# Table stage of a graph layer: 64-column score products, 19 row pairs ahead of sort group 1, and a new split of the row scaling between GpSimd and ScalarE

## The chip, the cores and the metric

One Trainium2 chip, one core of it. The metric is the device time of one execution in microseconds (us), taken as the median of several runs.

## What is computed

The reference is a graph layer followed by a feed-forward (slice attention) layer. There are 6250 nodes with 256 features and 106250 weighted edges, sorted by destination in the input arrays. What the change touches is the first half of the graph layer:

```python
support = layernorm(x) @ W
r_D = sigmoid(support @ a2)
gated = r_D * support
out = segment_sum(gated[col] * edge_values[:, None], row, num_segments=n)
sumnorm = segment_sum(edge_values * r_D[col, 0], row, num_segments=n)
```

All that follows (the division, the gating with softplus, the feed-forward layer) is untouched. Because the product with W is linear, the kernel leaves it to the end of the sum. It first builds a **table** with one row of 257 numbers for each node: the normalized features times the gate `r_D`, and the gate itself. It then gathers rows of that table for the edges and adds them up by destination.

## The kernel before

The 6250 rows are kept in on-chip memory as 49 blocks of 128 rows (`NB = 49`), and 25 pairs of blocks (`NPAIR`). Two things are made before the gathering can start, and they run interleaved on all engines.

**The table stage.** For each pair `p`:
- TensorE transposes the two blocks (`cross1`, L1823, four transposes that the profile puts under L1831), ScalarE copies them out of PSUM (`crossed1`, L1558, copy at L1563), and TensorE multiplies them with one column of weights (`support`, L1835), which gives one score for each row. These score products have one moving column; the profile puts them under the helper's line, L1766, as `bank<-S 128x1`. A pair has eight such records, as each float product is two.
- The pairs form four **chunks** (`CUTS`, L70): pairs 0 to 6, 7 to 12, 13 to 18 and 19 to 24, that is 14, 12, 12 and 11 blocks. For a chunk, VectorE scales the scores (`opened`, L1024, its product at L1027), ScalarE takes an exponential (`weight`, L1565, L1568), and VectorE turns them into gates, gains and shifts (`closed`, L1029, L1032 to L1035).
- Each block is then scaled by its gains into a ring of 18 row buffers, `Gt` (`GB = 18`, L67): even blocks by ScalarE (`scaled`, L1570, L1577 and L1578), odd ones by GpSimd (`scaled`, L781, L791 and L792). SyncE stores the blocks in their order, 0 to 48, to the table in DRAM (L641), and waits for each block's scaler. A block 18 or more reuses the buffer of the block 18 before it, so its scaler first waits until the **whole chunk** of that block is stored (`stored`, L568).

**The sort stage** sorts the edges into lists by destination block, in 26 groups of 32 columns. A group `g` goes through VectorE (`lookup` L992, `flag` L958, `place` L1012, `values` L974, `quad` L998, `later` L984, `hot` L1005, `mark` L969, in that order), TensorE (`quads` L1782, `total` L1808, `above` L1769, `other` L1778, and the two halves of `put`, L1793) and ScalarE (`runs_out` L1545 at L1550, `front` L1528 at L1533, `weigh` L1535 at L1542). GpSimd sends the result to DRAM by an indirect DMA (`send`, L756, L765). `other(g + 1)` on TensorE needs `front(g + 1)`, stands ahead of both halves of `put(g)`, and `lookup(g + 1)` on VectorE needs it too. `quads(g)` and `send(g - 1)` need `runs_out(g - 1)`.

**The order by hand.** The first 13 pairs (`FIRST`, L66) go through TensorE ahead of group 1 (L1897), the other twelve are spread over groups 1 and 2, six to a group, at six slots `pair(g, 0)` to `pair(g, 5)`. On VectorE, `pair` (L1037) opens chunk `g` at `(g, 0)` and closes it at `(g, 2)`, for g = 1, 2, 3; chunk 0 is opened and closed ahead of group 1, between the row statistics (L1098) and the second part of the reciprocal roots (`scales(1)`, L1111), which waits for ScalarE's `guess1(1)` (L1552). On ScalarE, after the first pairs, come `weight(0)` and `guess1(1)`, and then for each group:

```python
                pair(g, 0)
                if g > 1:
                    runs_out(g - 1)
                pair(g, 1)
                front(g + 1)
                for i in range(2, PER):
                    if i == 3:
                        weigh(g, 1)
                    pair(g, i)
```

Its `pair` (L1581) scales its half of chunk `g - 1` in the slots from `(g, 2)` on, and chunk 3 at `(3, 5)`. GpSimd's program is `send(0)`, chunks 0 and 1, `send(1)`, chunk 2, `send(2)`, chunk 3, `send(3)`.

**The end of the stage.** When `send(0)` to `send(3)` have landed, and behind the 49 stores in its queue, SyncE loads the first lists (`heads`, L644, L649). VectorE decodes them at the start of group 5 (`decode1`, L1148, L1143), and GpSimd begins to fetch table rows with them (`fetch1`, L769, L777). From there sorting of the later groups and a first pass of gathering and adding run together to about 550 us, and the rest of the gathering and the feed-forward layer follow.

Of the kernel before, what the change touches and what calls it, by code (L numbers as in the profile page):

```python
# [31 lines left out]
P = 128  # L32
N = 6250
F = 256
# [28 lines left out]
GS = (4, 10)  # L63
G1 = GS[0]
PER = 6
FIRST = 13  # L66
GB = 18  # L67
STARTS = (G1 + 1, 12)
NPAIR = -(-NB // 2)
CUTS = (0, 7, FIRST, FIRST + PER, NPAIR)  # L70
NCH = len(CUTS) - 1
assert FIRST + 2 * PER >= NPAIR
WG = 3
H = 8
G = 64
# [3 lines left out]
GW = F + 1  # L79
# [30 lines left out]
def build(nc, x, src, dst, ew, W, a1, a2, W_fx, b_fx, W_x, b_x, W_slice, b_slice, W_q, W_k, W_v,  # L110
          W_out, b_out, temp, out, gtab, srt, ovs):
    with ExitStack() as ctx:
# [305 lines left out]
        s_gt = [sem(f"s_gt{k}") for k in range(2)]  # L418
# [140 lines left out]
        def chunk(j):  # L559
            return 2 * CUTS[j], min(NB, 2 * CUTS[j + 1])  # L560

        def chunk_of(b):
            return sum(b // 2 >= c for c in CUTS) - 1

        def score_bank(j):
            return bank[7 - 4 * (j % 2)]

# [53 lines left out]
        def _(sp):  # L621
# [15 lines left out]


            for b in range(NB):
                sp.wait_ge(s_gt[b % 2], b // 2 + 1)  # L640
                sp.dma_start(gtab[b * P:(b + 1) * P, :], Gt[:, b % GB, :]).then_inc(s_gd[chunk_of(b)], 16)  # L641


# [99 lines left out]
        def _(pool):  # L743
# [12 lines left out]
            def send(g):  # L756
                k = g % 2
                if g == 0:
                    pool.wait_ge(s_zdma, 32)
                else:  # L760
                    pool.wait_ge(s_run, g * 16)
                pool.wait_ge(s_idx0, g + 1)
                pool.wait_ge(s_out, g + 1)
                pool.sem_inc(s_tick, 1)
                pool.indirect_dma_start(  # L765
                    srt[:, :], bass.IndirectOffsetOnAxis(ap=idx[:, k:k + 1], axis=0),
                    runs[k], None).then_inc(s_run, 16)
# [13 lines left out]
            def scaled(j):  # L781
                lo, hi = chunk(j)
                pool.wait_ge(s_gr, j + 1)
                pool.sem_inc(s_tick, 1)
                for b in range(lo, hi):
                    if b % 2 == 0:
                        continue
                    if b >= GB:
                        pool.wait_ge(*stored(chunk_of(b - GB)))
                        pool.sem_inc(s_tick, 1)  # L790
                    pool.tensor_copy(Gt[:, b % GB, F:GW], gate[:, b:b + 1])  # L791
                    pool.tensor_scalar(Gt[:, b % GB, 0:F], res[:, b, :], mean[:, b:b + 1], gain[:, b:b + 1],  # L792
                                       ALU.subtract, ALU.mult).then_inc(s_gt[1], 1)

            send(0)
            scaled(0)
            scaled(1)
            send(1)
            scaled(2)
            send(2)  # L800
            scaled(3)
            send(3)


# [95 lines left out]
        def _(dve):  # L900
# [123 lines left out]
            def opened(j):  # L1024
                lo, hi = chunk(j)
                dve.wait_ge(s_gm, CUTS[j + 1])
                v.tensor_tensor(score[:, lo:hi], score_bank(j)[:, lo:hi], nrs[:, lo:hi], ALU.mult).then_inc(s_g1, 1)  # L1027
# [7 lines left out]
                v.scalar_tensor_tensor(shift_[:, lo:hi], mean[:, lo:hi], -1.0, gain[:, lo:hi], ALU.mult, ALU.mult).then_inc(s_gr, 1)  # L1035

            def pair(g, i):  # L1037
                if g < NCH:
                    if i == 0:
                        opened(g)  # L1040
                    if i == 2:
                        closed(g)

            def dots():
                dve.wait_ge(s_w, 16 * len(wloads))
# [471 lines left out]
        def _(act):  # L1517
# [52 lines left out]
            def scaled(j, lo, hi):  # L1570
                act.wait_ge(s_gr, j + 1)
                for b in range(lo, hi):
                    if b % 2 == 1:
                        continue
                    if b >= GB:
                        act.wait_ge(*stored(chunk_of(b - GB)))
                    a.copy(Gt[:, b % GB, F:GW], gate[:, b:b + 1])  # L1577
                    a.activation(Gt[:, b % GB, 0:F], res[:, b, :], ACT.Identity,  # L1578
                                 bias=shift_[:, b:b + 1], scale=gain[:, b:b + 1]).then_inc(s_gt[0], 1)

            def pair(g, i):  # L1581
                if g < NCH and i == 1:
                    weight(g)
                if turn_of(g, i) < NPAIR:
                    crossed1(turn_of(g, i))
                if g < NCH:
                    lo, hi = chunk(g - 1)
                    if i >= 2:
                        scaled(g - 1, lo + (hi - lo) * (i - 2) // 4, lo + (hi - lo) * (i - 1) // 4)
                if g == NCH - 1 and i == PER - 1:  # L1590
                    scaled(g, *chunk(g))

            def evac(ns):
                for n in ns:
# [29 lines left out]
            for n in range(FIRST):  # L1624
# [2 lines left out]
                    runs_out(0)  # L1627
                if n == 4:
                    guess1(0)
            weight(0)  # L1630
            guess1(1)
            for g in range(1, G1 + 1):
                pair(g, 0)
                if g > 1:
# [129 lines left out]
        def _(pe):  # L1764
# [70 lines left out]
            def support(p):  # L1835
                j = chunk_of(2 * p)
                pe.wait_ge(s_pc, p + 1)
                if j >= 2:
                    pe.wait_ge(s_g1, j - 1)
                for k, b in enumerate(blocks(p)):  # L1840
                    o = score_bank(j)[:, b:b + 1]
                    mm(o, xT1[:, p % 2, k * F:k * F + P], Wg[:, 0, F:GW], True, False)
                    m = mm(o, xT1[:, p % 2, k * F + P:(k + 1) * F], Wg[:, 1, F:GW], False, True)
                m.then_inc(s_gm, 1)

            def step1(n):
# [353 lines left out]
```

## Time and profile before

| | us |
|---|---|
| median of 3 runs | 1389.09 |
| lowest and highest | 1387.78, 1393.01 |
| the profiled execution's own time | 1378.09 |
| its span, first to last instruction | 1376.3 |
| TensorE, VectorE, GpSimd, ScalarE busy | 1191.1, 1027.6, 881.7, 564.2 |

The rows further down are from the profiled execution. Times are us from the start of its span. An engine's row gives start, duration, engine, line, operation, the tiles written and read, their shapes and how many instructions were merged; in brackets stands how long the engine was idle before, and what ended the wait. The "granted clock" of TensorE is a share of its full speed of 2.4 GHz: 1.00 is 2.4 GHz and 0.50 is 1.2 GHz. Busy TensorE time includes time at either clock.

### The profile page before, as it was taken

How to read it: one execution, taken by the hardware profiler on the slowest of the kernel's cores; microseconds unless marked ns; L12 is line 12 of the kernel's file. 1: busy time of each engine (PE TensorE's matmuls, PEld its weight loads, DVE VectorE, ACT ScalarE, POOL GpSimd, SP SyncE). 2: the span in 40 equal slices, each digit the busy share in tenths (PEclk: the TensorE clock that was granted, in tenths of full speed). 3: DMA queues.
4: the chain of work that ended last, by engine and by line, in shares of the span. 5: the costliest groups of instructions: out<-in, count | busy, mean ns of one | idle time of the engine just before them, and what ended most of it. 6: DMA issues, size and time to landing. Idle time of an engine off the chain costs nothing.

```text
span 1376.3 us, 22834 instructions
## 1 busy us (share of the span) xinstructions
PE 1191.1 (87%) x6533; PEld 950.6 (69%) x6533; DVE 1027.6 (75%) x2618; ACT 564.2 (41%) x2046; POOL 881.7 (64%) x894
## 2 busy tenths in 40 slices
PE   3977688888888989789999998989898999988998
PEld 2976577787777888466766666656565666656887
DVE  8777899999898997717787776777777777775222
ACT  3254355555554445003444444443443434443232
POOL 0068777777777777767777777777777777760000
PEclk9677799999999999769999999999999999999999
DMA  8023455665555555736544446544444444441122
GB/s 268 19 70 100 68 150 150 145 165 138 146 147 144 154 135 142 141 93 124 132 129 121 128 130 119 135 120 127 122 128 124 125 126 119 128 112 36 39 76 72
DMA packets 163712, 166.74 MB, mean 121 GB/s; under 512 B 84709, under 2 KB 136185, under 8 KB 163596
## 3 DMA queue, kind: packets, MB, share of 16 engines
q0 software_dynamic: 39712, 108.02, 30.2%
q1 hardware_dynamic: 102716, 37.97, 11.8%
q10 hardware_dynamic: 21168, 19.35, 4.6%
q8 instruction: 54, 0.88, 0.3%
q14 instruction: 62, 0.51, 0.1%
HBM read 137.12 MB, written 28.14 MB: 120 GB/s over the span
## 4 chain that ended last, share of the span: by engine, by line
PE 47%; POOL 12%; issue 11%; DMA 10%; DVE 10%; ACT 8%; POOLq 1%; SPq 0%; ACTq 0%; DVEq 0%
PE bank L1766 45%; POOL rows L874 10%; DMA rows<-gated_rows_dram,ring_i 7%; ACT big L1542 5%; DMA overflow_sums_dram<-ovr 1%; POOL rows L792 1%; ACT big L1708 1%; DVE S L1330 1%; POOLq L866 1%; PE bank L2011 1%; PE bank L1831 1%; DVE lg L1359 1%; DVE big L963 1%; DVE hm L1354 1%; DVE neg L1371 1%
## 5 line engine op out<-in xcount | busy, mean ns | idle before, releaser
L1766 PE MATMUL bank<-rows,S 128*128 128x257 f32 (+1 forms) x2254 | 584.6, 392 | 58.2 <-DMA rows<-gated_rows_dram,ring_i 40.3
L874 POOL DMA_INDIRECT rows<-gated_rows_dram,ring_i x516 | 504.4, 977 | 165.6 <-issue 141.4
L1766 PEld LDWEIGHTS bank<-rows,S 128*128 128x128 f32 x2254 | 409.2, 193 | 183.9 <-DMA rows<-gated_rows_dram,ring_i 79.1
L777 POOL DMA_INDIRECT rows<-gated_rows_dram,lg x294 | 288.7, 982 | 99.8 <-issue 73.4
L1766 PE MATMUL bank<-big 128*104 128x128 f32 (+3 forms) x1824 | 227.1, 288 | 69.6 <-ACT big L1542 50.0
L1766 PEld LDWEIGHTS bank<-big 128*104 128x104 f32 (+2 forms) x1824 | 221.6, 193 | 79.8 <-issue 78.1
L1542 ACT ACTIVATE big<-big 128x52 f32<-128x52 bf16 x768 | 180.0, 324 | 13.6 <-ACT ovr L1601 13.6
L1330 DVE TENSOR_SCALAR S<-iota,lof,srec 128x128 f32<-128x128 f32 x588 | 163.3, 359 | 1.8
L1766 PE MATMUL bank<-xn,lg 128*128 128x256 f32 x392 | 100.1, 379 | 0.0
L1766 PE MATMUL bank<-Wxs,xT 128*128 128x512 f32 x196 | 97.2, 618 | 0.3 <-ACT xT L1695 0.3
L1601 ACT COPY ovr<-bank 128x257 f32<-128x257 f32 x98 | 36.1, 369 | 149.3 <-PE bank L1766 132.8
L1157 DVE TENSOR_SCALAR S<-iota,lg,srec 128x128 f32<-128x128 f32 x294 | 84.0, 360 | 4.5 <-PE bank L1766 3.0
L1766 PE MATMUL bank<-big,lg 128*128 128x128 bf16 (+3 forms) x623 | 60.6, 247 | 28.6 <-DVE big L966 13.3
L1766 PEld LDWEIGHTS bank<-xn,lg 128*128 128x128 f32 x392 | 74.1, 190 | 10.7 <-issue 0.5
L1009 DVE TENSOR_TENSOR big<-bank,lg 128x2048 f32<-128x2048 f32 (+1 forms) x40 | 75.4, 1884 | 0.0
L1371 DVE SCALAR_TENSOR_TENSOR neg<-ag,bc,a1b 128x256 f32<-128x256 f32 x49 | 23.8, 486 | 67.6 <-ACT ag L1660 67.6
L1766 PEld LDWEIGHTS bank<-big,lg 128*128 128x128 bf16 x623 | 47.9, 103 | 37.9 <-DVE big L963 12.9
L1341 DVE TENSOR_TENSOR ag<-bank,ovr 128x257 f32<-128x257 f32 x49 | 20.9, 426 | 67.7 <-PE bank L1766 42.5
L1507 DVE TENSOR_TENSOR S<-bank,res 128x256 f32<-128x256 f32 x49 | 20.8, 425 | 64.6 <-PE bank L1766 64.6
L1708 ACT ACTIVATE big<-bank,zcol 128x128 f32<-128x128 f32 (+1 forms) x196 | 68.2, 356 | 0.0
L1682 ACT ACTIVATE xn<-res,bc 128x256 f32<-128x256 f32 x49 | 29.4, 600 | 88.3 <-DVE bc L1397 88.3
L765 POOL DMA_INDIRECT sorted_edges_dram<-big,idx x26 | 30.7, 1182 | 53.5 <-issue 51.9
(271 smaller groups left out, 1547.0 us busy)
## 6 DMA issues: line engine op xcount, KB each, us to landing
overflow_sums_dram<-ovr ACTq DMA_DIRECT2D x98, 128.5 KB
rows<-gated_rows_dram,ring_i POOLq DMA_INDIRECT x516, 3.2
gated_rows_dram<-rows SPq DMA_DIRECT2D x49, 128.5 KB, 3.1
ovr<-overflow_sums_dram SPq DMA_DIRECT2D x49, 128.5 KB, 2.9
rows<-gated_rows_dram SPq DMA_DIRECT2D x49, 128.5 KB
out_dram<-S SPq DMA_DIRECT2D x48, 128.0 KB, 1.7
rows<-gated_rows_dram,lg POOLq DMA_INDIRECT x294, 3.1
res<-in_x_dram SPq DMA_DIRECT2D x1, 4352.0 KB
```

The lines of the kernel that those rows point to most:

```text
L765: pool.indirect_dma_start(srt[:, :], bass.IndirectOffsetOnAxis(ap=idx[:, k:k + 1], axis=0), runs[k], None).then_inc(s_run, 16)
L777: pool.indirect_dma_start(rows[:, turn(n), :], None, gtab[:, :], bass.IndirectOffsetOnAxis(ap=ring1[:, n:n + 1], axis=0)).then_inc(s_row[t ...
L874: pool.indirect_dma_start(rows[:, slot(b, u), :], None, gtab[:, :], bass.IndirectOffsetOnAxis(ap=ring_i[:, b // CH % 2, n:n + 1], axis=0)) ...
L1009: v.tensor_tensor(hot_s[h], r.unsqueeze(2).broadcast_to([P, HC, RUN[h]]), iota1[:, 0:RUN[h]].unsqueeze(1).broadcast_to([P, HC, RUN[h]]), A ...
L1157: v.tensor_scalar(S[:, turn(n), :], iota[:, :], lof1[:, n:n + 1], srec[:, 1, n:n + 1], ALU.is_equal, ALU.mult).then_inc(s_S, 1)
L1330: v.tensor_scalar(S[:, S_slot(b, u), :], iota[:, :], lof[:, b // CH % 2, n:n + 1], srec[:, 1, NT1 + b * TQ + u:NT1 + b * TQ + u + 1], ALU. ...
L1371: step(v.scalar_tensor_tensor(neg[:, :], ag[:, 0:F], col(RI), a1b[:, :], ALU.mult, ALU.mult, accum_out=col(ZD)))
L1542: m = a.activation(hot_v[h][:, j, 1, :], flagsj[g % 2][:, h, j, :], ACT.Copy, scale=ewf[:, n:n + 1])
L1601: a.copy(ovr[:, k, :], bank[6 + k][:, 0:GW]).then_inc(s_evac, 1)
L1682: a.activation(xn[:, b % 3, :], res[:, b, :], ACT.Identity, bias=col(NM), scale=col(RS)).then_inc(s_xn, 1)
L1708: m = a.activation(swt[:, c, b * P:b * P + n], turn_bank(b)[:, c * P:c * P + n], ACT.Identity, bias=zcol[:, 0:1], accum_out=nacc[:, c, b:b ...
L1766: return nc.tensor.matmul(o, l, r, start=start, stop=stop, skip_group_check=True)
```

## The change

- Score products have 64 moving columns (`WIDE`) in place of one: the same column of weights, read 64 times. The 63 further columns are overwritten by later blocks or not read.
- 19 pairs go through TensorE ahead of sort group 1, and the last six in group 1. The chunks stay as they are.
- VectorE opens chunks 1, 2 and 3 at `(1, 0)`, `(1, 3)` and `(2, 3)` and closes each two slots later; ScalarE's exponentials stand one slot after each opening. `weight(0)` and `guess1(1)` move up among the first pairs, behind pairs 12 and 16.
- GpSimd scales blocks 0 to 25 (chunks 0 and 1), ScalarE blocks 26 to 48 (chunks 2 and 3): chunk 2 in halves at `(2, 0)` and `(2, 1)`, chunk 3 in thirds at `(3, 0)`, `(3, 1)` and `(3, 2)`.
- GpSimd's program is now `send(0)`, chunk 0, `send(1)`, chunk 1, `send(2)`, `send(3)`.

```diff
@@ -63,13 +63,17 @@
 GS = (4, 10)
 G1 = GS[0]
 PER = 6
-FIRST = 13
+FIRST = 19
 GB = 18
+WIDE = 64
 STARTS = (G1 + 1, 12)
 NPAIR = -(-NB // 2)
-CUTS = (0, 7, FIRST, FIRST + PER, NPAIR)
+CUTS = (0, 7, 13, 19, NPAIR)
 NCH = len(CUTS) - 1
-assert FIRST + 2 * PER >= NPAIR
+SCALED = {(2, 0): (2, 0, 2), (2, 1): (2, 1, 2),
+          (3, 0): (3, 0, 3), (3, 1): (3, 1, 3), (3, 2): (3, 2, 3)}
+OPENED = ((1, 0), (1, 3), (2, 3))
+assert FIRST + PER >= NPAIR
 WG = 3
 H = 8
 G = 64
@@ -562,6 +566,13 @@
         def chunk_of(b):
             return sum(b // 2 >= c for c in CUTS) - 1
 
+        def lent_pool(b):
+            return b < 2 * CUTS[2]
+
+        def scaler(b):
+            k = int(lent_pool(b))
+            return s_gt[k], sum(int(lent_pool(c)) == k for c in range(b + 1))
+
         def score_bank(j):
             return bank[7 - 4 * (j % 2)]
 
@@ -637,7 +648,7 @@
 
 
             for b in range(NB):
-                sp.wait_ge(s_gt[b % 2], b // 2 + 1)
+                sp.wait_ge(*scaler(b))
                 sp.dma_start(gtab[b * P:(b + 1) * P, :], Gt[:, b % GB, :]).then_inc(s_gd[chunk_of(b)], 16)
 
 
@@ -783,7 +794,7 @@
                 pool.wait_ge(s_gr, j + 1)
                 pool.sem_inc(s_tick, 1)
                 for b in range(lo, hi):
-                    if b % 2 == 0:
+                    if not lent_pool(b):
                         continue
                     if b >= GB:
                         pool.wait_ge(*stored(chunk_of(b - GB)))
@@ -794,11 +805,9 @@
 
             send(0)
             scaled(0)
+            send(1)
             scaled(1)
-            send(1)
-            scaled(2)
             send(2)
-            scaled(3)
             send(3)
 
 
@@ -1035,11 +1044,10 @@
                 v.scalar_tensor_tensor(shift_[:, lo:hi], mean[:, lo:hi], -1.0, gain[:, lo:hi], ALU.mult, ALU.mult).then_inc(s_gr, 1)
 
             def pair(g, i):
-                if g < NCH:
-                    if i == 0:
-                        opened(g)
-                    if i == 2:
-                        closed(g)
+                if (g, i) in OPENED:
+                    opened(1 + OPENED.index((g, i)))
+                if (g, i - 2) in OPENED:
+                    closed(1 + OPENED.index((g, i - 2)))
 
             def dots():
                 dve.wait_ge(s_w, 16 * len(wloads))
@@ -1570,7 +1578,7 @@
             def scaled(j, lo, hi):
                 act.wait_ge(s_gr, j + 1)
                 for b in range(lo, hi):
-                    if b % 2 == 1:
+                    if lent_pool(b):
                         continue
                     if b >= GB:
                         act.wait_ge(*stored(chunk_of(b - GB)))
@@ -1579,16 +1587,14 @@
                                  bias=shift_[:, b:b + 1], scale=gain[:, b:b + 1]).then_inc(s_gt[0], 1)
 
             def pair(g, i):
-                if g < NCH and i == 1:
-                    weight(g)
+                if (g, i - 1) in OPENED:
+                    weight(1 + OPENED.index((g, i - 1)))
                 if turn_of(g, i) < NPAIR:
                     crossed1(turn_of(g, i))
-                if g < NCH:
-                    lo, hi = chunk(g - 1)
-                    if i >= 2:
-                        scaled(g - 1, lo + (hi - lo) * (i - 2) // 4, lo + (hi - lo) * (i - 1) // 4)
-                if g == NCH - 1 and i == PER - 1:
-                    scaled(g, *chunk(g))
+                j = SCALED.get((g, i))
+                if j is not None:
+                    lo, hi = chunk(j[0])
+                    scaled(j[0], lo + (hi - lo) * j[1] // j[2], lo + (hi - lo) * (j[1] + 1) // j[2])
 
             def evac(ns):
                 for n in ns:
@@ -1627,8 +1633,10 @@
                     runs_out(0)
                 if n == 4:
                     guess1(0)
-            weight(0)
-            guess1(1)
+                if n == 12:
+                    weight(0)
+                if n == 16:
+                    guess1(1)
             for g in range(1, G1 + 1):
                 pair(g, 0)
                 if g > 1:
@@ -1838,9 +1846,9 @@
                 if j >= 2:
                     pe.wait_ge(s_g1, j - 1)
                 for k, b in enumerate(blocks(p)):
-                    o = score_bank(j)[:, b:b + 1]
-                    mm(o, xT1[:, p % 2, k * F:k * F + P], Wg[:, 0, F:GW], True, False)
-                    m = mm(o, xT1[:, p % 2, k * F + P:(k + 1) * F], Wg[:, 1, F:GW], False, True)
+                    o = score_bank(j)[:, b:b + WIDE]
+                    mm(o, xT1[:, p % 2, k * F:k * F + P], Wg[:, 0, F:GW].broadcast_to([P, WIDE]), True, False)
+                    m = mm(o, xT1[:, p % 2, k * F + P:(k + 1) * F], Wg[:, 1, F:GW].broadcast_to([P, WIDE]), False, True)
                 m.then_inc(s_gm, 1)
 
             def step1(n):
```

## Rows read from the trace of the kernel before

**Rows 1.** Chain that ended last, 60 to 165 us: start, us, what
```profile
103.94 6.39 PE bank L1766 x32
...
123.88 4.82 POOL rows L792
...
143.81 3.35 DMA sorted_edges_dram<-big,idx
...
147.60 2.05 DMA srec<-sorted_edges_dram
```

**Rows 2.** Timeline of TensorE, 46 to 92 us: transposes, and a half of put
```profile
46.17 0.60 PE L1831 MATMUL bank<-ident,res 128*128 128x128 f32 x4
...
48.71 0.64 PE L1831 MATMUL bank<-ident,res 128*128 128x128 f32 x4
...
58.91 1.09 PE L1831 MATMUL bank<-ident,res 128*128 128x128 f32 x4
...
61.37 1.09 PE L1831 MATMUL bank<-ident,res 128*128 128x128 f32 x4
...
88.12 3.14 PE L1766 MATMUL bank<-big 128*104 128x80 f32 x32
```

**Rows 3.** Stretches: us; PE, PEld, DVE, ACT, POOL busy; granted clock; DMA; GB/s
```profile
50.00:51.00 1.00, 1.00 (x12) 1.00 (x11) 0.91 (x5) 0.34 (x1) 0.00 (x0) 1.00 0.00 0
...
52.00:53.00 1.00, 1.00 (x7) 1.00 (x6) 0.00 (x0) 0.00 (x0) 0.00 (x0) 0.50 0.00 0
```

**Rows 4.** Timeline of VectorE, 53 to 150 us
```profile
53.20 0.17 DVE L1027 TENSOR_TENSOR big<-bank,big 128x14 f32<-128x14 f32 x1 [1.81 <-PE bank L1766]
...
65.68 0.17 DVE L1032 TENSOR_SCALAR big<-big 128x14 f32<-128x14 f32 x1 [3.78 <-ACT big L1568]
...
69.03 1.89 DVE L994 TENSOR_TENSOR big<-big,bank 128x1664 bf16<-128x1664 bf16 x1
...
93.46 0.17 DVE L1027 TENSOR_TENSOR big<-bank,big 128x12 f32<-128x12 f32 x1 [7.06 <-PE bank L1766]
...
101.51 3.69 DVE L1009 TENSOR_TENSOR big<-big,lg 128x2048 f32<-128x2048 f32 x2
...
107.23 1.89 DVE L994 TENSOR_TENSOR big<-big,bank 128x1664 bf16<-128x1664 bf16 x1
116.04 0.17 DVE L1027 TENSOR_TENSOR big<-bank,big 128x11 f32<-128x11 f32 x1 [6.92 <-PE bank L1766]
...
149.77 0.17 DVE L1143 CAST big<-srec 128x8 int32<-128x8 f32 x1 [3.70 <-DMA srec<-sorted_edges_dram]
```

**Rows 5.** Timeline of GpSimd, 97 to 112 us
```profile
97.89 0.36 POOL L791 COPY rows<-big 128x1 f32<-128x1 f32 x1 [10.84 <-DMA gated_rows_dram<-rows]
...
101.28 4.84 POOL L792 TENSOR_SCALAR rows<-res,big 128x256 f32<-128x256 f32 x1
...
108.64 1.09 POOL L765 DMA_INDIRECT sorted_edges_dram<-big,idx  x1 [0.20 <-issue]
109.75 0.19 POOL L791 COPY rows<-big 128x1 f32<-128x1 f32 x1
...
111.10 0.17 POOL L791 COPY rows<-big 128x1 f32<-128x1 f32 x1
```

**Rows 6.** The stores of the table (writers of its tensor), 60 to 150 us
```profile
DMA to landing us min/median/max: 2.1/3.1/4.7
```

**Rows 7.** Timeline of ScalarE in group 2, 94 to 105 us
```profile
94.44 0.27 ACT L1550 COPY big<-bank 104x128 f32<-104x128 f32 x1
...
98.35 0.34 ACT L1533 CAST big<-bank 128x208 bf16<-128x208 f32 x1
...
99.64 0.19 ACT L1577 COPY rows<-big 128x1 f32<-128x1 f32 x1
...
100.23 0.17 ACT L1577 COPY rows<-big 128x1 f32<-128x1 f32 x1
...
100.82 3.74 ACT L1542 ACTIVATE big<-big 128x52 f32<-128x52 bf16 x16
```

## The prediction

> **What bounds the kernel now.** I read the chain of waits first, for the stretch that the change touches, and then one engine's timeline at a time. In the chain [rows 1] the sort's products on TensorE (32 records, 6.39 us) carry it through group 2. From 116 us on GpSimd's scaling carries it, one block of it 4.82 us long. Then comes send(3), 3.35 us from issue to landing at 147.2, and the load of the first lists. VectorE's timeline [rows 4] shows what that means: it waits 7.06 us for TensorE before it opens chunk 2, 6.92 us before it opens chunk 3, 3.78 us for the exponential of chunk 0, and at 149.77 us it decodes the first lists, 3.70 us late. All that comes after (the later sort groups, the gathering) starts from that decode and has no tie to anything earlier, so I take the time of the decode as the measure: each us it moves is a us of the whole. The reader is to see two things more. Pairs of blocks go through TensorE at two speeds [rows 2]: two pairs in 2.54 us at 46 us, 1.27 each, and one in 2.46 us at 59 us. In both the engine is busy without a gap, and what differs is the granted clock, 1.00 and then 0.50 [rows 3], 2.4 and 1.2 GHz. And GpSimd needs 1.35 us for a block when undisturbed (109.75 to 111.10), but 4.84 us for the one that overlaps VectorE's 3.69 us of `hot` [rows 4, 5].
>
> **Wide products and the first 19 pairs.** The one-column products of a pair go at the pace of their weight loads; a half of put with 80 columns and weights of 104 takes 3.14/32 = 0.098 us a record [rows 2], so 64 columns should fit under the load of 128 weights, and I cost them at 0. If that cover were missing, each of a pair's eight records would add its own excess over that load; no row shows one, and nothing speaks for a gain. Whether they hold the clock no row shows. The bounds are the put's case, full clock at 88 us, and the one-column case, half clock from 52 us. I take full clock, as 64 columns are nearer to 80 than to one. Then pairs 3 to 18 start at 46.17 and take 16 x 1.27 = 20.3 us, plus a last product, to about 67.5.
>
> - Chunk 0 is opened when pair 6 is through, at 52.3 in place of 53.2. The statistics behind it take 61.90 - 53.20 = 8.7 us [rows 4] (61.90 is 65.68 less its wait), to 61.0. The exponential stands behind pair 12 on ScalarE, at 46.17 + 9 x 1.27 + 1.2 (transposes, copy) = 58.8, so the 3.78 us wait is gone. Chunk 0 is closed by 61.8 (0.8 us, as before).
> - What is late next is `guess1(1)`, behind pair 16: 46.17 + 13 x 1.27 + 0.6 (transposes) + 1.1 (copy and two logarithm steps) = 64.5. From there to the end of lookup(1) VectorE needs what it needs now, 70.92 - 65.68 - 0.8 = 4.4 us: 69.0 in place of 70.9. **Gain 1.9 us.**
>
> **Group 1.** VectorE does a group in 15.7 us without its wait (93.46 to 109.12) [rows 4], here 0.8 more for a second closing, and it no longer waits 7.06 us for a chunk at the group's start: lookup(2) ends at 69.0 + 15.7 + 0.8 = 85.5. TensorE's pairs 19 to 24 end by about 92.
>
> **The scaling of chunk 0.** All 14 blocks are now GpSimd's, from 62.0. Undisturbed they need 14 x 1.35 = 18.9 us. Nine blocks took it from 66.7 (the closing of chunk 0) to 87.05 (97.89 less 10.84) [rows 5], 20.3 us with all of VectorE's group 1 beside them, so group 1 blocks GpSimd for 20.3 - 12.2 = 8.1 us. Group 2's flag and values now fall in the same stretch; I estimate 4.7 us from their share. The bounds are no blocking at all and twice the second share. I take 62.0 + 18.9 + 12.8 = 93.7, and 3.1 us and a little for the last store [rows 6]: chunk 0 is stored at 97.2.
>
> **ScalarE's first wait.** At `(2, 0)` it scales blocks 26 to 31, into buffers of chunk 0, so it waits until 97.2. Six blocks at 0.59 (99.64 to 100.23) [rows 7] are 3.5 us. Behind them stands `runs_out(1)`, 0.27 us, now done at 94.71 and then at 101.0: **6.3 us later**. For it wait quads(2) on TensorE and send(1) on GpSimd.
>
> **ScalarE's second wait, the core of my forecast.** At `(2, 1)` it scales blocks 32 to 37, into the buffers of blocks 14 to 19, and so waits for all of chunk 1 to be stored. But chunk 1 is GpSimd's, stands in its queue behind send(1), and send(1) waits for `runs_out(1)`, which ScalarE has just done. So from 101.0: send(1) 1.1 to 1.4 us (108.64 to 109.75) [rows 5], twelve blocks 16.2 us, 3.7 us in which `hot(2)` blocks GpSimd [rows 4], the last store 3.1 us [rows 6]: 125.4. The six blocks add 3.5 us, and only then comes `front(3)`, 0.34 us, done at 129.3. Now it is done at 98.69, 4 us after `runs_out(1)`; then it is 28 us after it. Behind it stand on ScalarE `weigh(2, 1)`, 3.74 us [rows 7], and the exponential of chunk 3 (0.2 us); on TensorE other(3) and both halves of put(2); on VectorE the closing of chunk 3 and lookup(3). VectorE's chain is 129.3 + 3.7 + 0.2 + 0.8 (closing) + 2.0 + 1.9 (mark and lookup) = 137.9. Now lookup(3) ends at 109.12 [rows 4]. **Loss so far 28.8 us.**
>
> **What comes back.** Group 3 has no 6.92 us wait and no closing: 15.7 - 0.8 = 14.9, to 152.8, against 116.04 + 15.66 = 131.7 now (the same group's length). Loss 21.1. TensorE's put(2), 6.4 + 3.1 from 129.4, and put(3) end ahead of what VectorE asks of them, so their clock costs nothing here. Group 4 now takes from 131.7 to 146.07 (149.77 less the wait of 3.70), 14.4 us, with 0.9 of waiting for send(2), which then lands early: 13.5, to 166.3. The lists are then there: put(3) ends about 157, send(3) follows at once as nothing stands ahead of it in GpSimd's queue, and 3.35 us and 2.4 us more (143.81 to 149.65) [rows 1] make 163. So the decode starts at 166.3 against 149.77. **Sum: 16.5 us slower**, of which 1.9 + 7.1 + 6.9 + 0.9 + 3.7 = 20.5 were gained and 37 lost in two waits. The profiled execution would take 1378.09 + 16.5 = 1394.6. The median is 11.0 us (0.8%) above it, and the forecast for the median is 1389.09 + 16.5 = 1405.6.
>
> **Rules weighed.** GpSimd's 4.84 us block began 0.23 us before `hot` at 101.51 [rows 4, 5] and was held up all the same. The Trainium skill (SBUF — State Buffer, Who interferes with whom) says that GpSimd and a VectorE instruction with two inputs in SBUF share a read port, that the one that starts first holds it to its end, and that ScalarE waits for nobody. That speaks against this change, which moves blocks from ScalarE to GpSimd; the trace agrees that GpSimd is the one to suffer, but not that the first to start is safe. By the rule the caught block would lose nothing, and the sum would be 0.4 us shorter. TensorE is busy 1.00 in both stretches of [rows 3], with the clock at 1.00 and at 0.50. The skill (TensorE: Matmul & The Clock Gate, Why this matters for your kernels) says that an engine kept continuously busy gets its full clock; the trace disagrees. By that rule alone, the wide columns would change nothing.
>
> **The rivals.**
> - *The clock falls all the same.* The pairs then take 2.46 us from 52 us on. For it speaks that half of a pair's work is still the same transposes. Against it, the put's case. Pair 16 comes 11 us later, lookup(1) ends at 84, group 1's put and the pairs behind it at 102, and `runs_out(1)` at 105.8 rather than 101.0; the rest follows: 4.8 us more, 1410.4.
> - *Faster: the second wait finds its chunk stored.* If the twelve blocks of chunk 1 were stored when ScalarE comes to `(2, 1)`, which decides at 101 us, nothing would hold front(3). VectorE would run groups 2 and 3 back to back and the lists would set the end; the gains, less the late `runs_out(1)`, are some 14 us: 1375. Against it stands the order of GpSimd's queue: chunk 1 can't start before send(1).
> - *No difference: the loss is made up.* VectorE and GpSimd might meet less than I took. With no blocking at all in chunk 0, TensorE's pairs (92) and ScalarE's six blocks set `runs_out(1)` to 95.5, 5.5 us earlier, and `hot(2)` gives 3.7 back: 7.3 us slower are left, 1396.4. Only with some slack after 150 us as well would it be a draw, about 1392. The chain [rows 1] shows no such slack, with VectorE, lists and GpSimd in line.
> - *Worse.* If GpSimd's blocks of chunk 1 took half as long again as undisturbed, 8 us more: 1414.
>
> **How the numbers follow.** I give the forecast 0.70, the fallen clock 0.12, worse 0.06, no difference 0.08 and faster 0.04. A measurement of this kernel tells about 0.5% (6.9 us) from no change. The range goes from the unblocked case to the worst one, 1396 to 1414, and leaves out the two cases that aren't slower and some of the edges. Faster by over 0.5% 0.04, within it 0.09, slower 0.87.
>
> **What would show it.** In the profile after: a granted clock of 1.00 from 50 to 68 us and 1.27 us a pair; no waits of VectorE of 7 us for its opening products (L1027's line of before) in groups 2 and 3; ScalarE's longest wait, 24 us, on a store of the table ahead of the second half of chunk 2, with TensorE and VectorE idle from about 108 to 129 us; GpSimd's twelve blocks in that stretch at 1.35 us each; the first lists decoded at 166 us without a wait for their DMA, and every later stage late by the same amount. It would be wrong if front(3) came within 10 us of `runs_out(1)`, if lookup(3) ended before 125 us, or if the delay at the decode were gone by the end of the first pass at 550 us.

## The result, and the profile after

| | before | changed |
|---|---|---|
| median of 20 runs, us | 1386.71 | 1391.45 |
| lowest and highest | 1378.9, 1393.01 | 1387.8, 1398.21 |
| the profiled execution's own time | 1378.09 | 1392.19 |
| its span | 1376.3 | 1390.4 |

The ratio is 1.0041, with a 95% interval of 1.0025 to 1.0057: about 5 us slower, within the 0.5% that I had called no change, and below the 1396 at which my range began. I had forecast 16.5 us slower. Yet between the two profiled executions the difference is 14.1 us, near the forecast. So there are two questions: whether the 14 us arise as I said, and why only 5 of them are left between the medians.

The pages give the granted clock in 40 slices of 35 us, first for the kernel before, then for the changed one:

```profile
PEclk9677799999999999769999999999999999999999
```

```profile
PEclk9985889999999999868999999999999999999999
```

The second and third slices (35 to 104 us), most of the table stage, now have 9 and 8 where they had 6 and 7; the 5 behind them is the long wait that follows below. The timeline of TensorE in the first 19 pairs:

```profile
48.72 0.61 PE L1839 MATMUL bank<-ident,res 128*128 128x128 f32 x4
49.16 1.00 PE L1774 MATMUL bank<-S 128*128 128x64 f32 x8
...
64.03 0.61 PE L1839 MATMUL bank<-ident,res 128*128 128x128 f32 x4
...
65.31 0.61 PE L1839 MATMUL bank<-ident,res 128*128 128x128 f32 x4
```

A pair takes 1.28 us at 64 us as at 48, where [rows 2] have 2.46 us at 59. The 64-column products cost nothing that counts: eight of them are busy 1.00 us, eight of one column 0.95 us, and at full clock a pair takes 1.28 us with either.

Then ScalarE, which answers to [rows 7] (start, duration, engine, line and tiles as ahead of the prediction):

```profile
96.56 0.19 ACT L1585 COPY rows<-big 128x1 f32<-128x1 f32 x1 [4.33 <-DMA gated_rows_dram<-rows]
...
100.08 0.24 ACT L1558 COPY big<-bank 104x128 f32<-104x128 f32 x1
124.08 0.19 ACT L1585 COPY rows<-big 128x1 f32<-128x1 f32 x1 [23.76 <-DMA gated_rows_dram<-rows]
...
127.60 0.31 ACT L1541 CAST big<-bank 128x208 bf16<-128x208 f32 x1
```

Both waits that I forecast are there: 4.33 us for the stores of chunk 0, then `runs_out(1)` (L1558) at 100.1, then 23.76 us for the stores of chunk 1, and `front(3)` (L1541) ends at 127.9. GpSimd, to [rows 5]:

```profile
101.33 1.09 POOL L776 DMA_INDIRECT sorted_edges_dram<-big,idx  x1 [6.92 <-ACT big L1558]
102.44 0.19 POOL L802 COPY rows<-big 128x1 f32<-128x1 f32 x1
...
120.55 1.21 POOL L803 TENSOR_SCALAR rows<-res,big 128x256 f32<-128x256 f32 x1
```

Send(1) goes out when `runs_out(1)` is done, and the twelve blocks follow it, to 121.8. VectorE, to [rows 4]:

```profile
66.97 0.20 DVE L1123 TENSOR_TENSOR big<-big 128x35 f32<-128x35 f32 x1 [3.72 <-ACT big L1564]
...
69.71 1.89 DVE L1003 TENSOR_TENSOR big<-big,bank 128x1664 bf16<-128x1664 bf16 x1
...
102.47 0.56 DVE L1010 TENSOR_REDUCE big<-bank 128x32 f32<-128x384 f32 x1 [8.91 <-PE bank L1774]
...
131.70 0.17 DVE L1041 TENSOR_SCALAR big<-big 128x11 f32<-128x11 f32 x1 [22.93 <-ACT big L1576]
...
134.38 1.89 DVE L1003 TENSOR_TENSOR big<-big,bank 128x1664 bf16<-128x1664 bf16 x1
...
163.65 0.17 DVE L1151 CAST big<-srec 128x8 int32<-128x8 f32 x1
```

Its two waits of 7 us are gone. Two of 8.9 us (for `quads(2)`, behind `runs_out(1)`) and 22.9 us (for the exponential of chunk 3, behind `front(3)`) have come, and the first lists are decoded at 163.7 without waiting for them. From there to the end of the program both profiled executions need the same: the own times less the decode are 1228.3 us before and 1228.5 after.

### The profile page after: what moved, and what is told of

Same layout as the page of the kernel before. It is cut to its first block, busy times and chain, and to the rows that moved or that the text cites. A ratio compares the mean times of both kernels' runs of the same rounds, so it can differ in the third digit from the quotient of the medians.

```text
span 1390.4 us, 22822 instructions
## 1 busy us (share of the span) xinstructions
PE 1186.4 (85%) x6533; PEld 948.3 (68%) x6533; DVE 1029.6 (74%) x2618; ACT 563.5 (41%) x2042; POOL 874.0 (63%) x898
## 4 chain that ended last, share of the span: by engine, by line
PE 42%; POOL 14%; DVE 11%; issue 11%; DMA 11%; ACT 8%; POOLq 1%; SPq 0%; ACTq 0%; DVEq 0%
PE bank L1774 40%; POOL rows L883 10%; DMA rows<-gated_rows_dram,ring_i 7%; ACT big L1550 5%; POOL rows L803 3%; DMA overflow_sums_dram<-ovr 2%; ACT big L1716 1%; DVE S L1338 1%; PE bank L2019 1%; POOLq L875 1%; DVE big L1018 1%; DVE big L988 1%; DVE big L972 1%; DVE big L979 1%; DVE lg L1367 1%
## 5 line engine op out<-in xcount | busy, mean ns | idle before, releaser
L1774 PE MATMUL bank<-big 128*104 128x128 f32 (+3 forms) x1824 | 230.7, 291 | 65.9 <-ACT big L1550 51.2
L1774 PEld LDWEIGHTS bank<-big 128*104 128x104 f32 (+2 forms) x1824 | 225.4, 196 | 75.0 <-issue 73.4
L1774 PE MATMUL bank<-big,lg 128*128 128x128 bf16 (+3 forms) x623 | 57.6, 240 | 57.0 <-ACT big L1541 25.3
L1774 PE MATMUL bank<-xn,lg 128*128 128x256 f32 x392 | 101.0, 382 | 0.0
L776 POOL DMA_INDIRECT sorted_edges_dram<-big,idx x26 | 32.8, 1262 | 91.4 <-issue 52.9
```

Of the source, the lines that this page charges most:

```text
L776: pool.indirect_dma_start(srt[:, :], bass.IndirectOffsetOnAxis(ap=idx[:, k:k + 1], axis=0), runs[k], None).then_inc(s_run, 16)
L1774: return nc.tensor.matmul(o, l, r, start=start, stop=stop, skip_group_check=True)
```

## The experiments

**Both kernels again.** The first question was what an ordinary execution of either kernel looks like.

> The kernel before, unchanged, profiled a second time. The first profile had the first lists decoded at 149.8 us and a time of 1378.1, while 20 runs spread from 1378.9 to 1393.0 around 1386.7. Theory A (the spread is made in the first 150 us, where six pairs of blocks and the sort products ran at half clock for a time that varies, and they set the pace there): another profile has the decode anywhere from 149 to 164 us and its own time moves with it, so that time minus decode stays within 2 us of 1228.3. Rival B (the spread is made later, in the gathering): the decode stays at 149.8 within 1 us and the time moves without it.

> The changed kernel, unchanged, profiled a second time. Its first profile had the decode at 163.7 us; its 20 runs spread less (1387.8 to 1398.2). Theory A (its first 150 us hang on GpSimd's and ScalarE's chain, not on TensorE's clock): decode at 163.7 within 1.5 us, time 1388 to 1394. Rival B: the decode stays too, and the time can be anywhere in the spread.

> The kernel before, unchanged, a third profile. The first two had the decode at 149.8 and 156.7 us, own times of 1378.1 and 1385.2, and a clock that rose again from 0.50 at 75 and at 90 us. Theory A (TensorE's clock in the first 100 us decides): the decode lies between 149 and 160 us, later the longer the clock stays at 0.50 between 33 and 100 us, and time minus decode is 1227 to 1232. Its usual value must be near 156, so that the median of some 1388 comes out. Rival B: a decode near 150 with a time above 1384.

> As before_3: a fourth profile of the kernel before, with the same expectations of both theories.

> The changed kernel, unchanged, a third profile. The first two had the decode at 163.7 and 164.7 us. Theory A (its first 150 us don't hang on the clock): 163 to 166 us again. Rival: a spread as wide as that of the kernel before, 7 us.

| kernel, profile | opening of chunk 2 | first decode | own time | own time less decode |
|---|---|---|---|---|
| before, first | 93.5 | 149.8 | 1378.1 | 1228.3 |
| before_2 | 97.4 | 156.7 | 1385.2 | 1228.5 |
| before_3 | 98.1 | 156.4 | 1395.8 | 1239.5 |
| before_4 | 97.2 | 157.1 | 1392.6 | 1235.5 |
| changed, first | | 163.7 | 1392.2 | 1228.5 |
| after_2 | | 164.7 | 1396.8 | 1232.1 |
| after_3 | | 164.0 | 1394.7 | 1230.7 |

The first profile of before, on which my prediction rests, differs from the other three, which have the decode 6.6 to 7.3 us later. How common each kind is, four profiles don't tell: of the 20 timed runs of before, six took 1378.9 to 1380.5 us and nine less than 1385, so executions as quick as that profile are not rare. The changed kernel's three profiles lie within 1.1 us at the decode. What differs shows in the table stage. The stretch from 33 to 100 us, in the first profile of before:

```profile
33.00:100.00 67.00, 61.03 (x430) 57.33 (x431) 50.84 (x118) 22.83 (x65) 23.59 (x23) 0.74 0.14 45
```

in before_2:

```profile
33.00:100.00 67.00, 63.59 (x394) 60.04 (x391) 46.89 (x107) 21.18 (x60) 21.47 (x19) 0.65 0.13 44
```

and in the changed kernel's first:

```profile
33.00:100.00 67.00, 53.84 (x450) 51.92 (x450) 51.16 (x118) 22.87 (x62) 32.14 (x29) 0.89 0.14 46
```

The column before the last two is the granted clock: 0.74, 0.65, 0.89. TensorE's timeline in before_2 tells where:

```profile
77.41 1.06 PE L1831 MATMUL bank<-ident,res 128*128 128x128 f32 x4
...
79.83 1.09 PE L1831 MATMUL bank<-ident,res 128*128 128x128 f32 x4
...
84.76 6.19 PE L1766 MATMUL bank<-big 128*104 128x128 f32 x32
```

In the first profile the clock had come back to 1.00 from 75 to 79 us, and three pairs of group 1 took 1.3 to 1.5 us each; here it stayed at 0.50 till 90, they took 2.4 us each, and the put behind them began at 84.8 in place of 81.2. VectorE waits for the pairs behind that put when it opens chunk 2. So half clock lies on the path of the kernel before, and hardly on that of the changed one.

That is not all of the 7 us, though; they arise in three places. Some 2.6 us (before_2; 3.5 and 2.8 in the others) are there when chunk 0 is opened, at 55.8 us in place of 53.2. The clock came back from 0.50 at 37 us in the first profile and at about 42 in the others, so that the first half of put(0), 32 records, went mostly at half clock and took 1.8 us longer. Here it is in before, then in before_2:

```profile
38.40 3.71 PE L1766 MATMUL bank<-big 128*104 128x128 f32 x32
```

```profile
38.46 5.46 PE L1766 MATMUL bank<-big 128*104 128x128 f32 x32
```

Only 1.0 to 1.3 us more come from there to the opening of chunk 2. The last 1.9 to 3.5 us come behind it, in GpSimd's queue: from send(2) to send(3), with five blocks of chunk 3 between them, it needs 14.9 us in the first profile and 18.0, 16.7 and 18.2 in the others. In before, then before_2:

```profile
128.91 1.83 POOL L765 DMA_INDIRECT sorted_edges_dram<-big,idx  x1 [0.21 <-issue]
...
143.81 1.42 POOL L765 DMA_INDIRECT sorted_edges_dram<-big,idx  x1 [0.21 <-issue]
```

```profile
133.00 1.83 POOL L765 DMA_INDIRECT sorted_edges_dram<-big,idx  x1 [0.20 <-issue]
...
150.98 1.08 POOL L765 DMA_INDIRECT sorted_edges_dram<-big,idx  x1 [0.21 <-issue]
```

The blocks meet VectorE's instructions at other moments there; whether they would do so without the late clock is not shown.

So Theory A holds for about 4 of the 7 us, and the rest is made in the same 150 us but not by TensorE's clock alone. It is wrong that all the spread is made there: before_3 and before_4 lose 11 and 7 us more behind the decode. Of before_3's, 8 are lost in the first pass, the decode to 574.2 us taking 417.8 us where the first profile has 409.7; the clock from 50 to 100 us behind the decode is 0.83 in it and 0.93 in the first profile. Nor is the changed kernel's own time as fixed as its decode: after_2 took 1396.8 us, above the 1388 to 1394 that I expected.

**One-column products in the changed kernel.**

```diff
-WIDE = 64
+WIDE = 1
```

> The changed kernel with one-column score products. The wide ones held the clock at 1.00 from 42 to 82 us in its profile, where the kernel before has 0.50 from 52 to 75 (first profile) or 90 us (second). If the width is what holds it: the clock falls in the first 19 pairs, lookup(1) ends at 78 to 85 us in place of 71.6, runs_out(1) comes 3 to 8 us later than 100.1, the decode at 167 to 171 us, and the time rises by 3 to 8 us against the changed kernel (1.006 to 1.010 of before). Rival (the order of the pairs holds the clock, or the delay vanishes in ScalarE's wait for the stores): decode and time as in the changed kernel within 2 us.

Measured: ratio to before 1.010 (1.0064 to 1.0136), median 1401.86 against 1391.45 for the changed kernel, decode 167.7. The clock fell to 0.50 at 57 us, among the first 19 pairs, and VectorE waited for ScalarE, first for the exponential of chunk 0 and then for `guess1(1)`:

```profile
66.30 0.17 DVE L1041 TENSOR_SCALAR big<-big 128x14 f32<-128x14 f32 x1 [2.91 <-ACT big L1576]
...
76.69 0.21 DVE L1123 TENSOR_TENSOR big<-big 128x35 f32<-128x35 f32 x1 [9.52 <-ACT big L1564]
```

The width holds the clock, not the order of the pairs. The decode moved by 3.5 us against the mean of the three profiles (164.1), within what I had bounded; the time by more, some 8 us by the ratios, and what the rest is I can't say from one profile.

**Wide products in the kernel before.**

```diff
+WIDE = 64
...
-                    o = score_bank(j)[:, b:b + 1]
+                    o = score_bank(j)[:, b:b + WIDE]
```

(and the weights' column broadcast to 64, as in the change).

> The kernel before with 64-column score products and nothing else. Theory A (half clock among the first pairs costs it time, by an amount that varies from run to run): clock 1.00 through the first 13 pairs, lookup(1) ends 4 us or more before 70.9, the decode at 145 to 150 us, a median 5 to 12 us under before (0.991 to 0.996), and a narrower spread. Rival (the end of the stage hangs on GpSimd's scaling and the stores, not on TensorE): decode 149 to 157 us and a ratio within 0.998 to 1.002.

Measured: ratio 0.9968 (0.9946 to 0.9991), decode 147.2, and the clock at 1.00 through the first 13 pairs. The gain in time is some 4 us, just short of the 5 to 12 that I expected, and the spread is not narrower (1377.4 to 1390.8 us in 12 runs). The decode is 9.5 us ahead of the 156.7 of the three later profiles, but that is not the width's alone. In this execution the clock came back at 37 us, as in the first profile of before, and chunk 0 was opened at 52.9. Against that profile the decode is 2.6 us earlier. How much of the 7 us between the profiles of before the width takes away is therefore not shown by the decodes; the times of the 12 runs say about 4 us. The waits of 6.7 and 7.1 us for the opening products remain. VectorE waits 5.1 us for the lists, behind GpSimd:

```profile
141.19 1.83 POOL L766 DMA_INDIRECT sorted_edges_dram<-big,idx  x1 [0.21 <-issue]
```

**The wait for chunk 1 by its queue.**

```diff
             scaled(0)
-            send(1)
             scaled(1)
+            send(1)
             send(2)
```

> The changed kernel, with GpSimd's send(1) behind its twelve blocks of chunk 1 in place of ahead of them. If ScalarE's wait at (2, 1) is this queue and nothing else: GpSimd, which sat idle 6.9 us for runs_out(1) and then sent for 1.1 us, begins chunk 1 at 94.5 in place of 102.4 and ends it 7 to 8 us earlier (some of its blocks meet VectorE's busy first part of group 2, so at least 6); front(3) comes at 120 to 122 us in place of 127.9, send(1) at about 115 costs nothing, the decode comes at 156 to 158 us in place of 163.7, and the ratio is 0.998 to 1.001. Rival (another wait, such as place(2) on the late send(1), takes its place): decode above 161 us.

Measured: ratio 0.9995 (0.9971 to 1.0019), decode 155.7. GpSimd's chunk 1 went from 94.8 to 113.7, and on ScalarE

```profile
116.09 0.19 ACT L1585 COPY rows<-big 128x1 f32<-128x1 f32 x1 [15.29 <-DMA gated_rows_dram<-rows]
...
119.61 0.31 ACT L1541 CAST big<-bank 128x208 bf16<-128x208 f32 x1
```

The wait is 8.5 us shorter, `front(3)` 8.0 us earlier and the decode 8.0 us earlier: each us of that wait is a us of the stage. In the time it is some 6 us by the ratios (0.9995 against 1.0041). This confirms the core of the forecast.

**The wait moved out of the way.**

```diff
-SCALED = {(2, 0): (2, 0, 2), (2, 1): (2, 1, 2),
-          (3, 0): (3, 0, 3), (3, 1): (3, 1, 3), (3, 2): (3, 2, 3)}
+SCALED = {(2, 0): (2, 0, 2), (3, 3): (2, 1, 2),
+          (3, 4): (3, 0, 2), (3, 5): (3, 1, 2)}
```

> The changed kernel, but ScalarE scales the second half of chunk 2 only at slot (3, 3), and chunk 3 at (3, 4) and (3, 5): front(3) no longer stands behind the wait for chunk 1's stores. The theory that this wait is the loss (27.5 us between runs_out(1) and front(3) in the profile, where the kernel before has 4): front(3) follows runs_out(1) within 4 us, ScalarE waits for the stores later, where nothing stands behind it but the rest of the scaling, lookup(3) ends near 114 us in place of 136.3, the first lists are decoded at 142 to 145 us in place of 163.7, and the time falls by about 20 us against the changed kernel, to 0.984 to 0.990 of the kernel before. Rival (the stage is bound by GpSimd's twelve blocks and the stores, whatever stands behind them): the decode stays above 155 us and the ratio to before stays above 0.998.

With `(2, 2)` in place of `(2, 0)` as well:

> As second_later, and the first half of chunk 2 moves from (2, 0) to (2, 2), behind runs_out(1) and front(3). In the profile of the changed kernel ScalarE waited 4.3 us for the stores of chunk 0 there and scaled for 3.5 us with runs_out(1) behind it, and VectorE sat idle 8.9 us for quads(2). If that first wait costs what it seems to: runs_out(1) at 92 to 94 us in place of 100.1, send(1) and chunk 1 some 7 us earlier, VectorE's wait at its reduction in group 2 under 2 us, decode at 136 to 140 us, and a further 4 to 7 us off against second_later. Rival (the end of the stage is then set by the stores of chunks 2 and 3 and the lists, which this edit doesn't move): the same as second_later within 2 us.

Measured: second_later has the decode at 157.4 and 1.0004 (0.9978 to 1.003), both_later at 153.9 and 0.9961 (0.9932 to 0.999). `front(3)` came 4 us after `runs_out(1)`, as said, but of the 20 us only 6 came back, and the ratio missed the 0.984 to 0.990 that I expected. In both_later `runs_out(1)` came at 94.2 us in place of the 99.4 of second_later, and the decode 3.5 us earlier still, far from the 136 to 140 us expected. Two other waits took the place of the one removed. VectorE in second_later:

```profile
137.41 0.22 DVE L1027 TENSOR_SCALAR big<-bank,big 104x2 f32<-104x2 f32 x1 [8.03 <-DMA sorted_edges_dram<-big,idx]
...
150.24 0.56 DVE L1010 TENSOR_REDUCE big<-bank 128x32 f32<-128x384 f32 x1 [9.29 <-PE bank L1774]
```

The first is for send(2), which stands in GpSimd's queue behind chunk 1. In the changed kernel that chunk ran while VectorE stood still; now VectorE works beside it, and the rows of GpSimd are

```profile
114.16 4.53 POOL L803 TENSOR_SCALAR rows<-res,big 128x256 f32<-128x256 f32 x1
...
118.98 3.57 POOL L803 TENSOR_SCALAR rows<-res,big 128x256 f32<-128x256 f32 x1
...
133.25 1.08 POOL L776 DMA_INDIRECT sorted_edges_dram<-big,idx  x1 [0.21 <-issue]
```

Twelve blocks take from 101.5 to 133.0, 2.6 us each, against 1.6 from 102.4 to 121.8. The second wait is for quads(4), behind `runs_out(3)`, which now has 17 blocks of ScalarE's scaling ahead of it and ends at 148.1. My expectation costed neither.

**The old split under the new order.** `lent_pool(b)` is `b % 2 == 1` again, and slots and GpSimd's queue are those of the kernel before; the wide products, the 19 pairs and the openings stay.

> The changed kernel (wide products, 19 pairs ahead, earlier openings), but odd blocks scaled by GpSimd and even ones by ScalarE, in the slots and the queue order of the kernel before. If the new split is the loss: no wait of ScalarE of more than 8 us on stores, no 7 us waits of VectorE for its opening products, and a decode between 140 and 150 us, held back by GpSimd, which works slower while VectorE works (2.6 us a block in second_later against 1.6 in the changed kernel): ratio 0.988 to 0.996. Rival (the earlier openings gain nothing, since GpSimd's scaling and the stores set the pace under any split): decode within 2 us of before_wide.

Measured: ratio 0.9939 (0.9914 to 0.9964), decode 144.5, own time 1375.2. Against the changed kernel, which differs from it in the split with its slots and queue order alone, the decode is 19 to 20 us earlier (2 to 3 of them there when chunk 0 was opened) and the time 1.0% shorter: the new split is the loss. Against before_wide, which has the same split, the decode is 2.7 us earlier, of which 1.1 us was there when chunk 0 was opened. VectorE's waits of 7 us for its openings are gone, but it waits 3.1 and 1.9 us for sends, and 7.2 us for the lists in place of 5.1:

```profile
144.52 0.17 DVE L1153 CAST big<-srec 128x8 int32<-128x8 f32 x1 [7.15 <-DMA srec<-sorted_edges_dram]
```

So the earlier openings take 13.8 us of waits from VectorE, and GpSimd's scaling ahead of the sends gives most of them back. At the end of lookup(4) VectorE is 5.4 us ahead of before_wide, at the decode 2.7. The intervals of the two ratios overlap.

**ScalarE scales everything.**

```diff
...
+SCALED = {(1, 0): (0, 7), (1, 1): (7, 14), (1, 4): (14, 18), (1, 5): (18, 22), (2, 2): (22, 26),
+          (2, 3): (26, 32), (2, 4): (32, 38), (3, 1): (38, 41), (3, 2): (41, 44), (3, 3): (44, 49)}
...
-            return b < 2 * CUTS[2]
+            return False
```

The pairs of numbers are first and last block here, and GpSimd only sends.

> The changed kernel with all 49 blocks scaled by ScalarE, 0.58 us each, 28 us in all, spread over ten slots of groups 1 to 3; GpSimd only sends. If the stage is held back by GpSimd's pace beside a busy VectorE (1.35 us alone, 2.4 to 2.7 beside it) and by the ring's waits on it: VectorE runs its groups without waits of more than 3 us, at 15 to 16 us a group, the decode comes at 133 to 140 us, and the ratio to before is 0.982 to 0.989, the best of all. Rival (ScalarE becomes the bound, with its exponents, front and weigh behind the scaling): decode above 150 us and ratio above 0.995.

Measured: ratio 0.9885 (0.9853 to 0.9917), median 1372.45 against 1389.25, decode 137.8: faster than both kernels. The profiled execution is one of its longer ones, 1378.2 us, with 1240.5 of them behind the decode. GpSimd no longer scales, and its sends go when `runs_out` allows:

```profile
94.79 1.01 POOL L776 DMA_INDIRECT sorted_edges_dram<-big,idx  x1 [45.34 <-ACT big L1554]
110.39 2.65 POOL L776 DMA_INDIRECT sorted_edges_dram<-big,idx  x1 [14.60 <-ACT big L1554]
129.10 2.42 POOL L776 DMA_INDIRECT sorted_edges_dram<-big,idx  x1 [16.06 <-ACT big L1554]
```

VectorE's longest wait in groups 1 to 4 is 5.40 us, for the exponential of chunk 3, which has ten blocks of scaling and the 3.7 us of `weigh` ahead of it on ScalarE, more than the 3 us I expected. ScalarE does not become the bound.

## Why the prediction was wrong

**The step that failed** is the last one, "the forecast for the median is 1389.09 + 16.5". It adds a shift worked out against one execution to a median that is 11.0 us above that execution, as if the 11 us had nothing to do with the change. Some of them do. In three further profiles of the kernel before the decode comes at 156.4 to 157.1 in place of 149.8. About 4 us of that are half clock, in a stage whose pace hangs on TensorE; the rest is made by GpSimd's blocks. The changed kernel's decode (mean 164.1) doesn't move with the execution, and against those three it is 7.4 us later, not 14 or 16.5.

From 1405.6 to the measured 1391.45 there are 14.2 us. Of these, 2.6 are the sum, which was too large (13.9 us was right for that execution), 2.4 are the median of before, 1386.71 us from 20 runs where I had 1389.09 from 3, and the remaining 9.2 are the step named.

The 7.4 us lie inside the interval of the measured difference (3.5 to 7.9 us), 13.9 and 16.5 don't. I can't resolve what is between 7.4 and 4.7: the first pass is some 2 us shorter in the changed kernel's profiles (decode to about 570 us: mean 410.6 us in three against 412.9 in four), but that is less than the spread within each kernel, and in how many of the timed runs of before the decode was early isn't known.

I had the sign of it in hand. I counted a gain of 1.9 us for the clock in the first pairs, and asked of half clock only what it would cost the changed kernel, not what it costs the kernel before in the executions that I hadn't seen.

**Point by point**, by the steps of the forecast, the first profiles compared:
- The clock stays at 1.00 through the first 19 pairs, 1.28 us a pair: right, and `narrow` shows that the width does it. Lookup(1) ends at 71.6, not 69.0. Pair 3 started 1.3 us later in that execution, at 47.4, and I had left out the ends of the chunks. At pairs 6 and 12 the products of two pairs follow each other and the next transposes wait, so that three pairs take 4.4 us in place of 3.8: 1.2 us in all before `guess1(1)`.
- Lookup(2) ends at 88.1 (forecast 85.5, with the same 2.6 us of offset). GpSimd ends chunk 0 at 94.4 (93.7), and the wait for its stores ends at 96.6 (97.2).
- `runs_out(1)` at 100.3 (101.0); the twelve blocks to 121.8 (122.3), the last store 2.3 us later (3.1 taken); `front(3)` at 127.9 (129.3).
- Lookup(3) ends at 136.3 (137.9), lookup(4) at 150.7 (152.8), the decode at 163.7 (166.3), without a wait for the lists. The sum against that profile was 13.9 us, not 16.5. I had let mark, lookup and the stores be too long, in small terms.
- Of ScalarE's two waits, the second is shown to be a loss by `chunk1_first`, where 8.5 us less of wait are 8.0 us at the decode. The first was moved only together with the second, in `both_later`, where `runs_out(1)` came 5.2 us earlier than in second_later and the decode 3.5 us.
- The rival of the fallen clock did not happen here; with one column it did, with lookup(1) at 81.7 (84 said), `runs_out(1)` at 104.3 (105.8), and the decode 3.5 us later (4.8 said). The rival of a loss made up is the outcome by its size, but not by its mechanism: GpSimd was blocked as I took it (31.0 us for chunk 0, 31.7 forecast), and no slack behind 150 us is shown. The kernel before is mostly slower than its profile was.
- The Trainium skill's rule on the shared port (SBUF — State Buffer, Who interferes with whom), that the one that starts first holds it: my reading that a block that started first was held up does not stand. Ahead of `hot` VectorE ran the second half of `later`, which also reads two inputs in SBUF, and it had begun 0.11 us before the block that starts at 101.28 in [rows 5]. The row is

```profile
101.17 0.42 DVE L989 TENSOR_TENSOR big<-big 128x512 bf16<-128x512 bf16 x1
```

In the changed kernel it is the same (79.21 us, the block at 79.25, 3.62 us long). And where a block did start first, VectorE was the one held up. In the changed kernel, with a `later` instruction that takes 0.69 us elsewhere:

```profile
102.61 1.22 POOL L803 TENSOR_SCALAR rows<-res,big 128x256 f32<-128x256 f32 x1
```

```profile
103.06 1.17 DVE L996 TENSOR_TENSOR big<-big 128x512 bf16<-128x512 bf16 x1
```

So these rows agree with the rule, and since the block was not the first, the 0.4 us that the prediction gave the rule would not have come off.

**Open.** The later stages spread by up to 11 us from execution to execution, and I haven't tested what makes them. Nor is it shown why the clock comes back at 37 and 75 us in one profile of the kernel before and at about 42 and 90 in three. Each of the variants has one profile, so differences of 1 to 3 us between their decodes can be the execution's.

## What to carry to other kernels

Ask of the profiled execution where it stands among the runs before adding anything to their median: if it is nearly a per cent off, profile the same kernel again, and look for a clock or a wait on the path that the change would take away. When work is split over two engines and a ring, write down for each wait of the ring which queue its releaser stands in, and behind what. And an engine that is freed may slow the one beside it: GpSimd's blocks took 1.6 us each beside a mostly idle VectorE and 2.6 beside a working one, and giving all of them to ScalarE, at 0.58, was the best of the three splits tried.

## What the hardware did that I had not expected

Three of four profiles of the same kernel differ from the fourth by 7 us in the first 150 us (decode at 156.4 to 157.1 against 149.8). The clock fell to 0.50 between 51 and 53 us, among the pairs with one-column products, in all four. When it came back, at 75 or at about 90 us, was a matter of the execution. 64-column products in their place held it at 1.00 from 44 to 80 us in all three profiles of the changed kernel, and from 44 to 78 us in five variants of it. They took no time of their own: eight records of 64 columns were busy 1.00 us, eight of one column 0.95, and a pair took 1.28 us with either.
